# Expert rows added into DRAM by a row of accumulating scatters, and stacked bias and matrix products

## What is computed

```python
x0 = einsum('bct,bcd->bdt', x, W[cond])             # a 32x32 matrix per batch, one of 16
# mixture of experts, 16 experts of 512 -> 128 -> 512, two per token
scores = softmax(x0 @ router_w + router_b) + router_bias
gate   = the two best scores within the two best groups, else 0
y = sum_e gate[:, e] * ((silu(x0 @ w1 + b1) * (x0 @ w2 + b2)) @ w3 + b3)
z = (silu(x0 @ sw1 + sb1) * (x0 @ sw2 + sb2)) @ sw3 + sb3      # shared, 512 -> 256 -> 512
x1 = x + y + z
# per channel: causal convolution with a kernel of length 512, masked by a length per batch
u  = conv(x1 * mask, k) + D * x1 * mask, times mask
# feed-forward of 512 -> 1024 -> 512 with a latent branch, layer norm
out = x1 + layernorm(relu(u @ up)**2 @ down + latent(u))
```

## Time and profile before

| what | us |
|---|---|
| median of three runs (339.92, 343.78, 339.97) | 339.97 |
| the profiled execution | 343.47 |
| its span, first to last instruction | 341.6 |
| PE busy (share of the span) | 324.8 (95%) |
| DVE busy | 187.4 (55%) |
| ACT busy | 115.3 (34%) |
| POOL busy | 109.8 (32%) |
| share of the chain of waits on PE, on DVE | 80%, 10% |

### The profile page before, as it was taken

The page is one execution under the profiler, slowest core; times in us unless marked ns, Lnnn a source line. Parts: engine busy times, 40 slices in busy tenths (PEclk is TensorE's granted clock), DMA queues, the critical chain, the costliest instruction groups (busy, mean ns, idle before and its releaser), DMA issues.

```text
span 341.6 us, 5497 instructions
## 1 busy us (share of the span) xinstructions
PE 324.8 (95%) x1945; PEld 245.8 (72%) x1945; DVE 187.4 (55%) x375; ACT 115.3 (34%) x199; POOL 109.8 (32%) x131
## 2 busy tenths in 40 slices
PE   8998899999999599999998899899999999999994
PEld 2566788988887288888686444468888787888872
DVE  3747896888365122365469469537322446442366
ACT  1571312323722123363006833832231424222120
POOL 8243004356577546663400000699200000000000
PEclk9999999999999879999999999999999999999999
DMA  6999920796686629999969986000000000100002
GB/s 194 327 405 405 384 70 13 221 316 205 188 269 219 199 69 328 317 318 378 406 236 412 388 279 216 2 1 0 2 0 0 3 0 31 63 31 0 2 21 101
DMA packets 32830, 59.93 MB, mean 175 GB/s; under 512 B 7213, under 2 KB 8081, under 8 KB 32804
## 3 DMA queue, kind: packets, MB, share of 16 engines
q1 hardware_dynamic: 25764, 48.95, 41.6%
q0 software_dynamic: 4992, 8.42, 7.2%
q10 hardware_dynamic: 2048, 2.21, 1.8%
HBM read 55.02 MB, written 12.40 MB: 197 GB/s over the span
## 4 chain that ended last, share of the span: by engine, by line
PE 80%; DVE 10%; issue 5%; POOL 2%; ACT 2%; DMA 1%; ACTq 0%; DVEq 0%; POOLq 0%
PE bank L1606 15%; PE bank L435 13%; PE bank L437 12%; PE bank L436 12%; PE bank L1574 7%; PE bank L1679 5%; PE bank L1568 4%; PE bank L1434 2%; DVE acc L1259 2%; PE bank L1688 1%; PE bank L1384 1%; PE bank L1466 1%; PE bank L1390 1%; PE bank L1509 1%; DVE osum L1307 1%
## 5 line engine op out<-in xcount | busy, mean ns | idle before, releaser
L1606 PE MATMUL bank<-xt,ew 128*128 128x128 f32 x496 | 62.4, 280 | 0.0
L1606 PEld LDWEIGHTS bank<-xt,ew 128*128 128x128 f32 x496 | 59.6, 196 | 0.8 <-issue 0.7
L639 POOL DMA_INDIRECT xg<-xrow,tokx x31 | 33.3, 1073 | 38.9 <-DVE tokx L1077 25.2
L646 POOL DMA_INDIRECT ytok<-yout,dstx x31 | 31.9, 1029 | 33.3 <-DVE yout L1189 20.3
L1348 DVE TENSOR_TENSOR sq<-rel 128x512 f32<-128x512 f32 x16 | 13.3, 834 | 37.0 <-ACT rel L888 37.0
L1574 PE MATMUL bank<-ew,bhid 128*128 128x512 f32 x62 | 31.7, 595 | 0.0
L792 ACT ACTIVATE xt<-bank 128x512 f32<-128x512 f32 x31 | 18.4, 598 | 31.9 <-PE bank L1568 24.6
L1568 PEld LDWEIGHTS bank<-ident,xg 128*128 128x128 f32 x124 | 15.1, 141 | 16.1 <-issue 14.0
L435 PE MATMUL bank<-ah,uph 128*128 128x512 f32 x64 | 25.2, 394 | 0.9 <-issue 0.9
L435 PE MATMUL bank<-dnh,sqh 128*128 128x512 f32 x64 | 25.2, 393 | 0.4
L436 PE MATMUL bank<-dnl,sqh 128*128 128x512 f32 x64 | 24.9, 390 | 0.0
(11 more groups left out here) (316 smaller groups left out, 619.5 us busy)
## 6 DMA issues: line engine op xcount, KB each, us to landing
ew<-in_L_ffn_ew SPq DMA_DIRECT2D x51, 256.0 KB
ew<-in_L_ffn_ew SPq DMA_DIRECT2D x21, 512.0 KB, 11.9
toep<-kpad SPq DMA_DIRECT2D x4, 1536.0 KB, 17.6
acc<-in_x SPq DMA_DIRECT2D x4, 512.0 KB, 7.2
xrow<-xstage ACTq DMA_DIRECT2D x4, 512.0 KB, 7.7
yg_lo<-ytok SPq DMA_DIRECT2D x4, 512.0 KB, 4.9
yg_hi<-ytok SPq DMA_DIRECT2D x4, 512.0 KB, 8.1
upraw<-in_L_ffn_up_w SPq DMA_DIRECT2D x1, 2048.0 KB, 14.3
```

The source lines that it names most:

```text
L639: pool.indirect_dma_start(xg[:, n % XGS, :], None, xrow, bass.IndirectOffsetOnAxis(ap=tokx[:, n:n + 1].bitcast(U32), axis=0), bounds_check ...
L646: pool.indirect_dma_start(ytok, bass.IndirectOffsetOnAxis(ap=dstx[:, n:n + 1].bitcast(U32), axis=0), yout[:, n % YOS, :], None, bounds_che ...
L1606: mm = pe.matmul(bank[2 + n % 2][:, w * P:(w + 1) * P], ew[:, ring(n), col + k * P:col + (k + 1) * P], xt[:, n % 2, k, :], start=(k == 0), ...
```

## The change

1. `ytok` has N rows. Once all eight b3 terms are in `acc`, SP stores `acc` (2 MB) to `ytok`. Each scatter then adds (`compute_op=ALU.add`) its block's rows, already times their gate, to rows `tokx`; a token stands in two blocks, so each scatter waits until the one before has landed, and the first for the store.
2. The gates come by slot: `hotg` (one-hot times gate) and 16 f32 products on PE after block 1 give `gsl`, and `y_copy` multiplies by it. `dstx` and its 16 products are gone; the list's other 16 + 16 become 16, eight after each product.
3. The read-back is one load of 256 KB per tile into `acc` and one addition; two of ACT's eight `u_t` copies go to DVE; HOLD is 2 and not used for tile 0.
4. b3: high and low halves are stacked at rows 0, 32 and 64 of one operand, so that one product per tile does what three did. Five tiles are done ahead of the loop, one after block 0, two after block 1. The dynamic bias of the later blocks moves two blocks back.
5. `wraw` is padded to 128 rows and `rep4` is four identities side by side: two full products in place of eight of 32 rows. WARM is 1. The length loads move to POOL's queue; POOL clears `xg` first, since skipped rows now count with a gate of 0.
6. After the convolution ACT's `dnh` copies all stand behind the last `ah` copy, and `fch` behind the third `sqh`.

```diff
-    ytok = nc.dram_tensor("ytok", [N * K, T], F32).ap()
+    ytok = nc.dram_tensor("ytok", [N, T], F32).ap()
...
+    def b3_late(n):
+        return ((B3_FRONT,), range(B3_FRONT + 1, NT))[n] if n < 2 else ()
...
+        sp.wait_ge(b3_added, NT)
+        sp.dma_start(ytok.rearrange("(i p) t -> p i t", p=P), acc[:, :, :]).then_inc(sums_out, 16)
         sp.wait_ge(c_done, 2 * SH)
-        sp.wait_ge(bx_done, 2)
+        sp.wait_ge(gsl_done, 1)
         for g in range(4, 6):
             static_pair(g, st_in[3])
...
         for i in range(NT):
-            sp.dma_start(rows_of(i), ytok[i * P * K:(i + 1) * P * K, :].rearrange("(p k) t -> p k t", k=K))\
-                .then_inc(rows_in(i)[0], 16)
+            sp.dma_start(acc[:, i, :], ytok[i * P:(i + 1) * P, :]).then_inc(rows_in(i)[0], 16)
...
         def scatter(n):
             pool.wait_ge(yout_ok, n + 1)
-            pool.indirect_dma_start(ytok, bass.IndirectOffsetOnAxis(ap=dstx[:, n:n + 1].bitcast(U32), axis=0),
-                                    yout[:, n % YOS, :], None, bounds_check=K * N - 1, oob_is_err=False)\
+            if n == 0:
+                pool.wait_ge(sums_out, 16)
+            else:
+                pool.wait_ge(ys_out[(n - 1) % YOS], 16 * ((n - 1) // YOS + 1))
+            pool.indirect_dma_start(ytok, bass.IndirectOffsetOnAxis(ap=tokx[:, n:n + 1].bitcast(U32), axis=0),
+                                    yout[:, n % YOS, :], None, bounds_check=N - 1, oob_is_err=False, compute_op=ALU.add)\
                 .then_inc(ys_out[n % YOS], 16)
...
+            for row in (B3_ROWS[0], B3_ROWS[2]):
+                act.activation(gth[row:row + G, j * HALF:(j + 1) * HALF], bank[4 + j][0:G, :], ACT.Copy).then_inc(gt_ok, 1)
...
-                for j in range((g - NCG + 2) * JC // 2, (g - NCG + 3) * JC // 2):
-                    act.activation(dnh[:, j, :], dnraw[:, j, :], ACT.Copy).then_inc(dnh_ok, 1)
+        act.wait_ge(dn_in, 16)
+        for j in range(JC):
+            act.activation(dnh[:, j, :], dnraw[:, j, :], ACT.Copy).then_inc(dnh_ok, 1)
...
+        picked(gk[:, :, :], sc[:, :, :])
+        tt(hotg[:, :, :], f(hotb[:, :, 1, :]), pairs(gk[:, :, :], NSLOT), ALU.mult).then_inc(hotg_ok, 1)
         shared_hid(3)
-        for i in range(NT):
+        for i in range(B3_FRONT):
             add_b3(i)
...
-            dve.tensor_copy(yout[:, n % YOS, :], bank[6 + n % 2][:, :]).then_inc(yout_ok, 1)
+            dve.tensor_scalar(yout[:, n % YOS, :], bank[6 + n % 2][:, :], gsl[:, n:n + 1], None, ALU.mult).then_inc(yout_ok, 1)
...
-        dve.wait_ge(b3_added, NT)
-        for i in range(NT - 2):
+        for i in range(NT):
+            dve.wait_ge(*rows_in(i))
             add_y(i)
-        for n in range(K * NT):
...
+        for i in U_DVE:
+            copy_u(i)
...
-            split3(pe, bank[B3BANK[i % len(B3BANK)]][:, :], lambda _: (gth[:, s], gtl[:, s]),
-                   lambda _: (b3h[:, :], b3l[:, :]), 1).then_inc(b3_done, 1)
+            pe.matmul(bank[B3BANK[i % len(B3BANK)]][:, :], gth[:, s], b3h[:, :], start=True, stop=True).then_inc(b3_done, 1)
...
+            for i in b3_late(n):
+                b3_term(i)
+            if n == 1:
+                pe.wait_ge(hotg_ok, 1)
+                for m in range(K * NT):
+                    mm = pe.matmul(bank[6][:, 0:NSLOT], f(hotp[:, m, :]), hotg[:, m, :], start=(m == 0),
+                                   stop=(m == K * NT - 1))
+                mm.then_inc(gsl_done, 1)
```

More of the change, by code:

```diff
@@ L76, in adaln_ffn_program @@
     AHEAD_TILES = 2
-    HOLD = 3
-    WARM = 2
-    LIST_STEP = 4
+    HOLD = 2
+    WARM = 1
+    LIST_STEP = 8
     XGS = 4
@@ L258, in adaln_ffn_program @@
     gth = at(small, "gth", [P, N], F32R)
+    zrow = f(gth[3 * C:4 * C, 0:P])
     gam = at(r, "gam", [P, T])
     bet = at(r, "bet", [P, T])
-    r3 = list(small)
     b3p = at(small, "b3p", [P, T])
-    b3l = at(r3, "b3l", [P, T], F32R)
-    b3m = b3p[0:G, :]
     b3h = at(small, "b3h", [P, T], F32R)
@@ L289, in adaln_ffn_program @@
     gk = at(small, "gk", [P, K, NT])
-    dstx = at(small, "dstx", [P, NSLOT], I32)
+    gsl = at(small, "gsl", [P, NSLOT])
     tokb = at(small, "tokb", [P, NT])
@@ L480, in _ @@
         sp.wait_ge(drowz_ok, 1)
[L481 to L484, removed]
+        for row in B3_ROWS:
+            sp.dma_start(b3p[row:row + 1, :], sb3.rearrange("(o n) -> o n", o=1)).then_inc(l1_in, 16)
+            sp.dma_start(b3p[row + SH:row + G, :], eb3).then_inc(l1_in, 16)
         sp.dma_start(drow[LI - 1:P:P // KQ, :], d_param.rearrange("(o n) -> o n", o=KQ)).then_inc(l1_in, 16)
@@ L597, in _ @@
                            0.0, None, ALU.mult).then_inc(gates_ok, 1)
-        pool.tensor_scalar(gtl[:, :].rearrange("p (i n) -> p i n", n=P), prow[:, :].unsqueeze(1).broadcast_to([P, NT, P]),
-                           0.0, None, ALU.mult).then_inc(gates_ok, 1)
+        for j in range(BT):
+            pool.dma_start(leni[j * B:(j + 1) * B, :], length.rearrange("(b o) -> b o", o=1)).then_inc(len_in, 16)
         def split_hi(n):
@@ L835, in _ @@
         for i in range(NT - 1):
-            act.wait_ge(xt_done, i + 1)
-            copy_u(i, 0, KC)
+            if i not in U_DVE:
+                act.wait_ge(xt_done, i + 1)
+                copy_u(i, 0, KC)
         act.wait_ge(xt_done, NT)
@@ L891, in _ @@
                 act.activation(sqh[:, v % 2, :], sq[:, v % 2, :], ACT.Copy).then_inc(sqh_ok, 1)
+                if v == 2:
+                    act.activation(fch[:, :, :], fcraw[:, :, :], ACT.Copy).then_inc(fch_ok, 1)
                 if v == 0:
@@ L1097, in _ @@
         dve.tensor_copy(eji[:, :], ejf[:, :]).then_inc(eji_ok, 1)
-        picked(gk[:, :, :], sc[:, :, :])
         def gate_low():
@@ L1386, in _ @@
         pe.wait_ge(const_ok, IDENT)
+        pe.wait_ge(warm_ok, 3)
+        pe.wait_ge(rep_ok, 1)
         pe.wait_ge(wraw_in, 16)
         for w in (6, 7):
-            for b in range(BT):
-                mm = pe.matmul(bank[w][b * C:(b + 1) * C, :], ident[0:C, 0:C],
-                               wraw[:, :, :].rearrange("c k d -> c (k d)"), start=True, stop=True)
-            mm.then_inc(wall_done, 1)
+            pe.matmul(bank[w][:, :], rep4[:, :],
+                      wraw[:, :, :].rearrange("c k d -> c (k d)"), start=True, stop=True).then_inc(wall_done, 1)
         def transpose_mixed(i):
@@ L1595, in _ @@
         transpose_x(1)
-        for i in range(B3_EARLY, NT):
+        for i in range(B3_EARLY, B3_FRONT):
             b3_term(i)
@@ L1660, in _ @@
             pe.wait_ge(y_added, i + 1)
-            for _ in range(HOLD):
+            for _ in range(HOLD if i else 0):
                 pe.matmul(bank[YBANK[i]][:, :], hidh[:, 0, 0:P], sw3h[:, 0:T], start=True, stop=True)
-            pe.wait_ge(comb_ok, K * (i + 1))
             for k in range(KC):
```

136 lines of the change are left out of this document (68 added, 68 removed).

## The result

The changed kernel took 422.11 us (median of 4 runs, 420.04 to 422.78), the kernel before 339.95 in the same comparison: a ratio of 1.234, 95% interval 1.227 to 1.241. The forecast was 372, its range 345 to 410. The direction was right and the time was not: the number is one that rival B gave (412 to 450), which had 0.13. The profiled execution took 422.2, its span is 420.0. In some executions, whatever the kernel, the cores show a lower granted clock and the time is some per cent longer, so medians and ratios here are of the other runs alone.

What follows compares the result with a forecast made beforehand. The prediction took PE to bound the loop (3.09 us a block) and the read-back and DVE the 18.0 us after it. Chain +37.2, read-back -6.0, clock +1.5, after the convolution -0.9: +31.8 on 339.97, say 372; range 345 to 410.

Steps and rivals of the forecast that it cites:

- rival B: Scatter chain: a full read of 3.3 before each write, beat 5.5 to 6.7, time 412 to 450; chance 0.13.
- What sets the pace: Expert loop: its beat can't be shorter than one scatter's start-to-landing plus POOL's restart, with PE's gathers queued behind.
- I take B = 4.2: Scatter chain: time per link, between 2.8 and 6.7; 31 beats put the read-back at 211.3, +37.2 us.
- Latency, not bytes, is the price: Scatter chain: a scatter moves only about 136 KB, as rows of empty slots are skipped, so latency sets its cost.
- The fullness corrects itself: Expert loop: a longer beat spreads weight loads, bringing the second half's DMA share of 0.95 near the first's 0.80.
- Start of the chain: Before the first add: bias sums done at 68.9, store of acc 7.9, POOL's restart 0.78, so 77.6.
- rival D: Store of acc beside weights of blocks 8 to 11: 15.4 instead of 7.9, time 379; counted within the forecast's 0.67.
- POOL's small operations: Between scatters 7 and 8: they now stand inside the chain, 7.7 from scatter to scatter, 3.5 over the beat.
- Read-back to convolution: After the loop: one smaller load and one addition per tile make this stretch 12.0 instead of 18.0, -6.0 us.
- The clock: PE: upper level expected in the loop; a fall expected before the read-back, charged 1.5 us.
- Rival C: Expert loop: PE's waits lower the clock for good, a block takes 6.2, time near 425; chance 0.06.
- Rival A: Expert loop: the chain hides at a beat of 3.09 or less, time 335; chance 0.14, including beats up to 3.4.

Runs made afterwards that it cites:

- add_free: Changed kernel with adds into two rows per token, no wait for landings, only even rows read back; 346.4 us, ratio 1.013 to the kernel before.
- two_rows: Changed kernel with two rows per token, plain scatters without the chain, no store of sums, both rows read back and added; 343.2 us, ratio 1.006.
- plain_chain: Changed kernel with each scatter overwriting rows of ytok instead of adding, order and waits kept; 380.3 us, ratio 1.117 to the kernel before.
- skip_rows: Changed kernel with the scatter's bound at row 0, so hardly any row is added, waits kept; 386.8 us.

## Why the prediction was wrong

- *What sets the pace* was right: the loop beats by a scatter's landing, PE waits for gathers queued behind it, and no time is lost elsewhere. `add_free` and `two_rows` show it from both sides.
- *"I take B = 4.2: the 3.40 of the nearest row, and 0.8 for the read and for the queues being fuller"* is the step that failed: this term, the price of one link of the chain, measured 6.00. The 3.40 was about right as a quiet plain link (3.57 full, 2.89 empty), partly by luck. The 0.8 should have been 2.6. Against `plain_chain`'s 4.60 the add costs 1.4; the other 1.2 is what a loaded loop of plain scatters costs over 3.40. By `skip_rows` the same 2.6 is 1.4 for what runs beside the chain, 1.2 for the rows, and nothing else, since a quiet add without rows takes 3.45. From the first add to the read-back it took 259.08 - 76.26 = 182.8 us where 31 x 4.2 + 3.5 = 133.7 were forecast; less the 1.3 by which it started sooner, that is the 47.8. The mean lies within the bounds of 2.8 and 6.7 (single beats reach 10.12); between ends that far apart the value was taken from the row of a plain write, and the read of the add was all but left out.
- *"Latency, not bytes, is the price"* holds for the plain scatter (0.7 for 128 rows) and not for the add (1.95), and the 136 KB beside it is a mean that hides full blocks of 262 KB and empty ones.
- *"The fullness corrects itself"* is right for the mean and wrong for the price. The DMA share did fall, to 0.71 in the window of 144 to 191 us. But the loads come in bursts, and a landing beside the Toeplitz loads takes 8 to 9 us: from first to last scatter these loads alone cost 12, the loop's weights about 10 (two runs of one execution each, never both changes at once). A mean share doesn't show that.
- *POOL's longer instruction* was not in the sum at all: 0.6 per add, shown by `skip_rows`. It is within the 1.4 by which the add is dearer than a plain scatter.
- *Start of the chain*, 77.6 against 76.26; the store took 8.71 with weights behind it, near the lower end taken, so rival D did not happen.
- *POOL's small operations*: with the 3.5 charged over 4.2 that beat was to be 7.7, and it is 8.06, in `skip_rows` and in the changed kernel.
- *Read-back to convolution*: -6.0 forecast, 12.5 - 18.0 = -5.5 measured. *From the convolution on*: -0.9 forecast, -1.0 measured. The clock did fall before the read-back (0.50 in the window of 252 to 262 us); the 1.5 charged for it does not show as a loss of its own.
- *The clock*: the upper level was expected in the loop and did not hold. Rival C, a fall that sets the pace at 425, is not what happened: with the clock held up by filler it is still 412.
- *Rival B* had the right number by a partly wrong way. Its B of 5.5 to 6.7 was to come from a full read of 3.3 before each write. Quiet, the add costs 1.9 over a plain scatter with all rows and 0.6 without any; less than half of the 2.6 missing per beat are rows, more than half is what runs beside the chain.
- *Rival A* fell: even a plain scatter needs 3.57, over the 3.18 from which the chain would have hidden. The figure named beside it (the Trainium skill, "DMA: Bandwidth & Descriptors", section "Anatomy of one DMA — SWDGE (gpsimd) path": 2.0 us fixed plus bytes) gave an estimated 3.1 with a restart, for the mean of 136 KB. For the blocks as they are it gives an estimated 2.8 empty and 3.4 with 262 KB; the plain scatters measured 2.9 and 3.57, so the trace agrees for them, and the adds measured 3.5 and 5.4.

## What to carry to other kernels

A row of dependent DMAs is priced by its round trip, landing plus restart, times its length; here even an empty link cost 2.9 us. If that is longer than the loop's beat, give each scatter rows of its own and sum at the end, or take turns over two tensors. Price an accumulating scatter as its own operation (with all rows valid, half as much again as a plain one here). Look at what single links move and not at the mean, and multiply any uncertainty per link by the number of links before choosing a range. A chain of landings also turned bursts of loads into lost time: in `two_rows`, with the same loads and no chain, the scatters start 3.06 to 3.09 apart all the way from 125.7 to 165.8 us, Toeplitz loads included.

## What was not expected of the hardware

- An adding scatter of 128 rows, 262 KB, lands in 4.6 us where a plain one takes 2.75 (2.7 against 2.07 without rows), and holds the DMA engines three times as long for the same bytes (12.6 against 4.2 us times 16 for 1.57 MB).
- POOL's instruction for it takes 1.56 instead of 0.98 us even when nearly all rows are skipped.
- One landing grows from 4.6 to 9.3 us beside loads of 1.5 MB, at a mean DMA share of only 0.73.
- Holding PE's clock up with idle products made the kernel about 2% faster, though PE was waiting; most of the gain came where the Toeplitz loads lie, and by what way stays open.
